# Three pooled PSUM banks for the transposes and side products of an attention kernel, assigned by a table, and back transposes in odd steps

## The reference, cut to what matters

```python
x = LN(x + L0(x))        # gated neighbour sum, all batches at once
x = LN(x + L1(x, adj))   # 4 heads + 1 output layer: softmax(mask(h h^T)) h
x = LN(x + L2(x, adj))   # softmax(mask(leaky(left_i + right_j, 0.01))) h
x = LN(x + L3(x, adj))   # the same with slope 0.2
```

## Time and profile before

| | us |
|---|---|
| median of 3 runs | 5713.18 (5706.15 to 5714.59) |
| the profiled execution | 5713.95 |
| its span, first to last instruction | 5712.2 |
| PE busy | 5265.8 (92%) |
| DVE busy | 4372.0 (77%) |
| ACT busy | 3731.8 (65%) |
| POOL busy | 1942.3 (34%) |
| mean granted clock of TensorE | 0.978 of full |

### The profile page before, as it was taken

One profiled execution on the slowest core, in us unless ns is written; L12 is line 12 of the kernel. 1 busy time (PEld: TensorE's weight loads), 2 busy tenths in 40 slices (PEclk: granted clock), 3 DMA queues, 4 the chain that ended last, 5 costly groups with the idle time before them and its releaser, 6 DMA issues.

```text
span 5712.2 us, 132229 instructions
## 1 busy us (share of the span) xinstructions
PE 5265.8 (92%) x52922; PEld 4508.6 (79%) x52922; DVE 4372.0 (77%) x7325; ACT 3731.8 (65%) x5501; POOL 1942.3 (34%) x1724
## 2 busy tenths in 40 slices
PE   8499999999999899999999999999999999999966
PEld 6388787888878788887878878787888878788755
DVE  5677678778787877778787787878788787877866
ACT  3266557676676757667576666767576675767665
POOL 3400025133341523325241343415233252413466
PEclk9799999999999999999999999999999999999988
DMA  5200000000000000000000000000000000000000
GB/s 177 61 16 11 18 9 9 9 14 14 9 9 11 17 12 7 9 18 12 15 5 10 17 14 9 9 11 16 11 9 9 18 12 15 5 9 18 13 1 5
DMA packets 138241, 95.95 MB, mean 17 GB/s; under 512 B 96032, under 2 KB 115104, under 8 KB 137632
## 3 DMA queue, kind: packets, MB, share of 16 engines
q1 hardware_dynamic: 137632, 87.49, 6.1%
HBM read 35.55 MB, written 8.91 MB: 8 GB/s over the span
## 4 chain that ended last, share of the span: by engine, by line
PE 67%; issue 12%; DVE 6%; POOLq 6%; DVEq 2%; ACT 2%; POOL 1%; DMA 0%; SPq 0%; ACTq 0%
PE po L1067 22%; PE tp L1042 22%; PE pss L1030 9%; PE pss L1031 9%; POOLq L257 6%; DVE pt L1333 3%; DVE rows L1321 2%; PE px L988 2%; DVEq L257 1%; PE px L1055 1%; PE px L1005 1%; ACT rows L1234 1%; PE px L969 1%; PE px L1015 0%; POOL shut L866 0%
## 5 line engine op out<-in xcount | busy, mean ns | idle before, releaser
L1042 PE MATMUL tp<-ident,rows 128*128 128x128 f32 x14336 | 1948.1, 278 | 234.5 <-DVE pt L1333 193.3
L1333 DVE COPY pt<-tp 128x512 f32<-128x512 f32 x2048 | 1332.8, 686 | 921.1 <-PE tp L1042 912.1
L1234 ACT ACTIVATE rows<-rows,nm 128x2048 f32<-128x2048 f32 x896 | 1795.0, 2003 | 323.3 <-DVE nm L1321 321.2
L1042 PEld LDWEIGHTS tp<-ident,rows 128*128 128x128 f32 x14336 | 1600.9, 141 | 476.8 <-issue 308.2
L1067 PE MATMUL po<-pt,hn 128*64 128x128 f32 x28672 | 1782.8, 278 | 37.5 <-ACT ot L1195 36.3
L1067 PEld LDWEIGHTS po<-pt,hn 128*64 128x64 f32 x28672 | 1568.5, 138 | 192.4 <-issue 191.7
L1186 ACT COPY pt<-tp 128x512 f32<-128x512 f32 x1536 | 837.9, 589 | 769.7 <-PE tp L1042 760.9
L869 POOL TENSOR_TENSOR rows<-sr,mask 128x2048 f32<-128x2048 f32 x256 | 1048.7, 4098 | 514.7 <-PE tp L1042 508.4
L1030 PE MATMUL pss<-ha 128*128 128x512 f32 x2560 | 1062.9, 415 | 13.1 <-DMA ha<-hb 12.0
L1031 PE MATMUL pss<-ha,hb 128*128 128x512 f32 x2560 | 1009.5, 394 | 0.0
L1321 DVE CUSTOM_DVE_ANT_0 rows<-pss,mask,nm 128x1024 f32<-128x1024 f32 x640 | 821.7, 1284 | 88.2 <-issue 3.5
(11 more groups left out here) (108 smaller groups left out, 3220.6 us busy)
## 6 DMA issues: line engine op xcount, KB each, us to landing
hb<-ha SPq DMA_DIRECT2D x164, 128.0 KB, 2.3
ha<-hb SPq DMA_DIRECT2D x164, 128.0 KB, 2.3
adjb<-in_adj SPq DMA_DIRECT2D x32, 512.0 KB, 5.6
xin<-x SPq DMA_DIRECT2D x36, 128.0 KB, 2.5
xb<-in_x SPq DMA_DIRECT2D x16, 256.0 KB, 3.0
x<-t SPq DMA_DIRECT2D x16, 256.0 KB, 2.4
xb<-x SPq DMA_DIRECT2D x8, 512.0 KB, 4.0
out<-xb SPq DMA_DIRECT2D x32, 128.0 KB, 1.9
```

What stands on the lines that cost most here:

```text
L1042: last = nc.tensor.transpose(tp[q % 2][:, r * P:(r + 1) * P], rows[:, row.slot, jb * P:(jb + 1) * P], ident[:])
L1234: nc.scalar.activation(rows[:, row.slot, :], rows[:, row.slot, :], ACT.Exp, scale=-1.0, bias=nm[:, row.place, 1:2], accum_out=rs[:, row.pl ...
L1333: nc.vector.tensor_copy(pt[:, CH * q:CH * (q + 1), row.k % SLOTS, :], tp[q % 2][:].rearrange("p (j n) -> p j n", n=P)).then_inc(pt_dve, 1)
```

## The change

`tp0`, `tp1` and `px` become a pool `ring` of three banks; PSUM is as full as before. `place_in_banks` walks once over the whole program, with a guessed time for each use (how long PE takes for it, how long until it is copied), and gives each the bank that by this guess came free first. PE waits only for the copy of that bank's last user. Back transposes go one step later, into odd steps, and all that follows from them too: `finish`, `bend_block`, `la` to `ld`, `ra`, `rb`, and in the first layers `xt`, `h`, `r`. `low`, `proj` and `hn` keep their steps. For heads, `take_sums` writes straight into `zt`, where POOL multiplies in place, so it no longer waits for POOL. The tasks ahead of the first step become a segment of their own.

```diff
-TAIL = 8
+TAIL = 9
-END_GAP = 9
+END_GAP = 10
+BANKS = 3
+SIDE = ("xn", "xt", "proj", "hn", "h", "r")
...
+    def uses(self):
+        for s in self.steps:
+            row, turned = self.row(s), self.row(s - 2)
+            yield None, (1900 if row and row.gat else 0), 0
+            for key in self.side_uses(s):
+                yield key, 600, 1300
+            for q in (0, 1):
+                if turned:
+                    yield ("turn", turned.k, q), 440, 900
+            yield None, 1950 * bool(self.odd(s - 3) or self.odd(s - 4)), 0
+            if self.back(s):
+                yield ("back", self.back(s).pair), 150, 2600
+            for key in self.side_uses(s + 0.5):
+                yield key, 600, 2600
+            for q in (2, 3):
+                if turned:
+                    yield ("turn", turned.k, q), 440, 1100
...
     def back(self, step):
-        return self.odd(step - 5)
+        return self.odd(step - 6)
     def finished(self, step):
-        return self.odd(step - 6)
+        return self.odd(step - 7)
...
         for unit in (ADD1, ADD2):
             end = at(order, unit, n + CH - 1)
-            tasks += [(end + 7, "ra", unit, c), (end + 8, "rb", unit, c)]
+            tasks += [(end + 8, "ra", unit, c), (min(end + 9, 2 * len(order) + AHEAD - 1), "rb", unit, c)]
...
+def place_in_banks(segments):
+    now, free = 0, [0] * BANKS
+    for segment in segments:
+        for key, taken, held in segment.uses():
+            if key is None:
+                now += taken
+                continue
+            bank = free.index(min(free))
+            now = max(now, free[bank]) + taken
+            free[bank] = now + held
+            assert key not in segment.bank
+            segment.bank[key] = bank
...
-        tp = [ctx.enter_context(nc.psum_tensor(f"tp{i}", [P, BANK], F32)) for i in range(2)]
+        ring = [ctx.enter_context(nc.psum_tensor(f"ring{i}", [P, BANK], F32)) for i in range(BANKS)]
         po = ctx.enter_context(nc.psum_tensor("po", [P, BANK], F32))
-        px = ctx.enter_context(nc.psum_tensor("px", [P, BANK], F32))
...
-                    nc.gpsimd.tensor_tensor(dst, ot[:], ob[:].rearrange("p r n -> p (r n)"), ALU.mult)
+                    nc.gpsimd.tensor_tensor(dst, dst, ob[:].rearrange("p r n -> p (r n)"), ALU.mult)
...
             def take_sums(row):
-                if row.pair or back_c.n:
-                    used = out_c if where[0].behind_head(row) else back_c
-                    wait(used, used.n + row.pair)
                 wait(pv_c, pv_c.n + row.pair + 1)
+                if row.unit < H:
+                    nc.scalar.copy(zt[:, row.unit, row.t // 2, :], po[:, 0:P]).then_inc(ot_ready, 1)
+                    return
+                if row.pair or back_c.n:
+                    wait(back_c, back_c.n + row.pair)
                 nc.scalar.copy(ot[:], po[:, 0:P]).then_inc(ot_ready, 1)
...
-                    finished = segment.row(s - 7)
+                    finished = segment.row(s - 8)
```

More of the change, by code:

```diff
@@ L115, in __init__, with side_uses @@
             self.tasks.setdefault(step, []).append((name, unit, c))
-        assert all(k == "before" or int(k) in self.steps for k in self.tasks), self.tasks.keys()
+        assert all(int(k) in self.steps for k in self.tasks), self.tasks.keys()
+        self.bank = {}
+    def uses(self):
[15 more added lines that the diff above has]
+                    yield ("turn", turned.k, q), 440, 1100
+    def side_uses(self, key):
+        return [task for task in self.tasks.get(key, []) if task[0] in SIDE]
     def tasks_at(self, step):
@@ L162, in prologue @@
     order = [pair for u, hn in ((0, 1), (1, 2), (2, 1), (3, 2)) for pair in pairs_of(u, hn)] + [None] * GAP
-    tasks = [("before", "xn", 0, c) for c in range(NC)]
-    tasks += [("before", name, 0, g) for g in range(2) for name in ("proj", "low", "hn")]
+    tasks = []
     for u in range(H - 1):
@@ L173, in prologue, with start @@
     return Segment(order, False, True, tasks)
+def start():
+    tasks = [(0, "xn", 0, c) for c in range(NC)]
+    return Segment([], False, False, tasks + [(0, name, 0, g) for g in range(2) for name in ("proj", "low", "hn")])
 def next_head(first):
@@ L1034, in turn @@
             def turn(row, q):
-                if q >= 2:
-                    wait_copy(row, q - 2)
-                elif row.before:
-                    wait_copy(row.before, q + 2)
+                tile = take("turn", row.k, q)
                 for r in range(CH):
                     jb = CH * q + r
-                    last = nc.tensor.transpose(tp[q % 2][:, r * P:(r + 1) * P],
+                    last = nc.tensor.transpose(tile[:, r * P:(r + 1) * P],
                                                rows[:, row.slot, jb * P:(jb + 1) * P], ident[:])
                 last.then_inc(tr_ready, 1)
+                count = copied[row.copier[q]]
+                give(count, count.n + row.count[q] + 1)
             def turn_back(row):
@@ L1073, in run_segment @@
             def run_segment(segment):
-                for task in segment.tasks.get("before", ()):
-                    run_task(*task)
+                where[0] = segment
                 for s in segment.steps:
@@ L1134, in next_of, with tile_of @@
                 wait(count)
+            where = [None]
+            def tile_of(*key):
+                return ring[where[0].bank[key]]
             def run_task(name, unit, c):
```

97 lines of the change are left out of this document (50 added, 47 removed).

## The result

| | before | after |
|---|---|---|
| median, us | 5713.06 (5706.15 to 5714.59, 5 runs) | 5739.09 (5731.19 to 5742.19, 5 runs) |
| span of the profiled execution, us | 5712.2 | 5740.3 |
| PE busy, us | 5265.8 | 5303.1 |
| DVE busy, us | 4372.0 | 4439.0 |
| mean granted clock | 0.978 | 0.968 |

The change made the kernel slower: 1.0048 times the time before, with a 95% interval of 1.0037 to 1.006. The prediction, 5655 us and faster with a chance of 0.83, had the wrong sign, and its range ended 41 us short of the result. (All times here are of undisturbed executions; one of 8962 us, at a granted clock of 0.64, is left out of a median in experiment 7.)

The account below looks back on a forecast made before the run. Outside stretches paced by POOL or ACT, PE was taken to lose time in transposes waiting for DVE's copies. Terms sum to 8.3 us a turn, 58 in seven; + 2 - 1 = 59 off 5713.95 gives 5655 us (5635 to 5670, 50%).

Parts of the forecast that it names:

- (2) of what the change costs: Steps 48 and 56: `hn` now needs group 2's bank and waits for its copy, behind `low` and bend: -2.0 us a turn.
- Odd additive steps: Nine odd additive steps outside the POOL-bound stretch: third bank lets sums stand 0.5 us earlier each, +4.5 us a turn.
- `ra` at 45, 53 and 61: `ra` goes one step later, under dot products, so DVE's copies come sooner at three steps: +3.9 us a turn.
- `la` and `ld`: Pairs move from even to odd steps, where the third bank doesn't help: -1.0 us a turn, from 0 to -3.
- Repeats at 65 and 85: Groups 2 and 3 share one bank at these steps, so the second comes later: -2.2 us a turn.
- Step 91: `proj` gets a bank ACT emptied earlier, saving its 2.43 us wait and slow sums: +3.3 us a turn, 1.3 to 3.9.
- Steps 100 to 111: POOL's wait for transposes behind late `proj` and PE's wait for `ra` shrink: +1.8 us a turn, 0 to 3.5.
- (c): Rival: norm tasks and `low` outlast dot products in odd steps, some ten places of 1.5 us: 5739 us, chance 7%.
- (e): Rival: PE's clock swings in the additive steps, eight stretches with 1.5 us more each: 5739 us, chance 2%.
- (a): Rival: the stretch of `ADD2` steps paced by POOL loosens too, its term 6.5 us a turn: 5622 us, chance 15%.
- (b): Rival: DVE takes the place of the freed bank waits, halving the +4.5 and +3.9 terms: 5685 us, chance 17%.
- (d): Rival: gains of 5 and losses of 5 cancel, or the table is in effect the old one: 5713 us, chance 9%.

Follow-up runs that it names:

- experiment 7: Kernel before with the pooled banks, heads' sums straight into `zt`, norm tasks one step later and `xt`, `h`, `r` of `ADD1` 1 to 1.5 later: 5636.0 us.
- Experiment 3: Changed kernel with `proj`, `low` and `hn` of head 2 three steps later, at 49 to 51 and 57 to 59, table made anew: 5679.9 us.
- Experiment 4: Changed kernel with `hn` of head 2 given the back transpose's bank instead of the bank of transposes' group 2: 5730.0 us.
- experiment 6: Changed kernel with each POOL mask of L911 issued as two instructions of 1024 columns: 5704.0 us.
- experiment 2: Changed kernel with its moved steps but without the bank table: groups of transposes keep two banks in turn, all else the third: 5826.9 us.
- experiment 1: Kernel before with the pool of banks and its table, all steps as before, heads' sums straight into `zt`: 5678.7 us, ratio 0.994.

## Why the prediction was wrong

**The failed step is (2) of what the change costs, steps 48 and 56: with the gains at 49 and 57, a loss of 1.0 us a turn was predicted, and 13.1 measured.** The chain in it was right: `hn` waits for the bank of group 2, DVE has `low` and the bend ahead of that copy. The duration was wrong: I priced `low` as in the earlier trace rows, where it finds POOL idle, and didn't ask where POOL's mask would be. The change moves `finish` out of the gap between two masks; that move is listed with the change, and the prediction doesn't follow it on POOL. Experiment 3 prices it: with head 2's `proj`, `low` and `hn` elsewhere, 59 us come back. Experiment 4 gives `hn` alone 9 of them, and experiment 6, where only the masks are cut, takes back 35. This term is 12.1 of the 12.5 us a turn between forecast and result; the errors of all others cancel, by luck.

The rule for it was in the prediction. The Trainium skill, "GPSIMD Engine Reference", section 1, says that GpSimd contends with VectorE instructions that read two SBUF inputs. The traces agree, with 4.46 and 3.83 us for `low` of 0.69. I applied it to the one instruction that already was slow in the trace before, the bend of the earlier trace rows, and not to the others of its kind that the change shifts against POOL.

**Odd additive steps**: +3.5 predicted for the seven, +2.9 measured. The mechanism holds: an odd step starts 0.72 us earlier, 0.17 of it because the back transpose has left the step before. At 38, 42, 54 and 62, however, 0.51 us are given back: 0.17 is the back transpose, and most of the rest a wait of groups 2 and 3 for ACT's copy, which I had put at nothing. It is the first row here, of step 41 (0.25 us). The rows behind it are steps 44 and 45, where the wait of 0.51 us of the earlier trace rows stands only at 1590.69, and the 16 transposes across the border of the steps, in one row, wait for nothing:

```profile
1577.65 0.68 PEld L1088 LDWEIGHTS ring<-ident,rows 128*128 128x128 f32 x6 [0.25 <-ACT pt L1239]
...
1590.69 1.16 PE L1088 MATMUL ring<-ident,rows 128*128 128x128 f32 x8 [0.51 <-DVE pt L1390]
...
1593.83 2.17 PE L1088 MATMUL ring<-ident,rows 128*128 128x128 f32 x16
...
1598.54 0.42 DVE L1361 TENSOR_TENSOR xb<-xb,y 128x256 f32<-128x256 f32 x1
```

**`ra` at 45, 53 and 61**: right. The 1.80 us of the earlier trace rows are gone, and these steps start 1.3 us earlier than the other odd ones. `ra` (1598.54) stands in the next step, under dot products.

**`la` and `ld`**: a loss of 1.0 predicted, a gain of 3.8 measured by step 32. I looked only at where these tasks go and not at what they leave. In the kernel before, PE waits 3.8 us a turn in steps 8 to 31, at four places: at step 16 0.59 us for ACT's copy of what `h` has just made, since a new unit begins there; at 21 and 29 `proj` and `hn` 0.69 each, until ACT has emptied `px`; and at 23 1.84 for DVE's copies. After the change 0.4 are left. The longest of the four is the tasks' own: in step 22 DVE has `ld`, `la` (its first instruction is L1291) and `low` ahead of the copies; after the change it has `lc` and `low`. Before, then after:

```profile
1468.42 0.46 DVE L1291 SCALAR_TENSOR_TENSOR y<-y 128x256 f32<-128x256 f32 x1
...
1470.94 0.85 DVE L1284 TENSOR_TENSOR ha<-hc,hb 64x512 fp32r<-64x512 f32 x1
...
1471.82 1.29 DVE L1333 COPY pt<-tp 128x512 f32<-128x512 f32 x2
...
1472.66 1.16 PE L1042 MATMUL tp<-ident,rows 128*128 128x128 f32 x8 [1.86 <-DVE pt L1333]
```

```profile
1470.68 1.29 DVE L1390 COPY pt<-ring 128x512 f32<-128x512 f32 x2
...
1472.23 1.04 PE L1088 MATMUL ring<-ident,rows 128*128 128x128 f32 x8
```

The wait at 16 goes because `h` moves to the step behind it:

```profile
1425.77 1.09 PE L1042 MATMUL tp<-ident,rows 128*128 128x128 f32 x8 [0.59 <-ACT hn L1168]
```

By step 31 the moved steps alone (experiment 2) gain 2.6 us, the banks alone 0.5: most of this gain is the moved tasks', and experiment 7 keeps it. The range of the term, 0 to -3, had no reason to end at nothing on the upper side.

**Repeats at 65 and 85**: right, 1.2 us each. The eight transposes break into two groups of four with the wait between:

```profile
1721.73 0.60 PE L1088 MATMUL ring<-ident,rows 128*128 128x128 f32 x4
1723.18 0.66 PE L1088 MATMUL ring<-ident,rows 128*128 128x128 f32 x4 [0.85 <-DVE pt L1390]
```

**Step 91**: +3.3 predicted, +1.7 measured. `proj` lost its wait of 2.43 us and the sums behind it run at 1.97 us, as foreseen. But the 1.48 us for slow sums were read from one turn and counted in all seven. Before the change the wait of 2.43 stands in every turn, and the sums behind it are slow (3.2 to 3.5 us) in the second, third and fourth only; in the others they took 1.97. And the sums of step 90 now wait for ACT, and so does the transpose behind the next back transpose:

```profile
1876.14 1.97 PE L1115 MATMUL po<-pt,hn 128*64 128x128 f32 x32 [0.56 <-ACT zt L1246]
...
1879.06 1.09 PE L1037 MATMUL ring<-xz,wts 64*64 64x128 f32 x16
...
1883.83 0.44 PE L1088 MATMUL ring<-ident,rows 128*128 128x128 f32 x2 [0.49 <-ACT pt L1239]
```

**Steps 100 to 111**: +1.8 predicted, with 0 as the lower end; -1.3 measured. POOL's masks wait less for transposes, 336.0 us in the whole program in place of 508.4, and the bend is again 2.85 us long under a mask. What the lower end left out is where it now stands: ahead of the copies of groups 2 and 3, and `proj` of step 108 has group 2's bank. Before, the transposes of step 107 waited 2.10 us behind the bend; now `proj` waits 2.71.

```profile
1976.60 4.08 POOL L911 TENSOR_TENSOR rows<-sr,mask 128x2048 f32<-128x2048 f32 x1
...
1978.11 2.85 DVE L1397 SCALAR_TENSOR_TENSOR zt<-zt 128x256 f32<-128x256 f32 x1
...
1980.88 1.28 DVE L1390 COPY pt<-ring 128x512 f32<-128x512 f32 x2
...
1981.62 6.41 PE L1037 MATMUL ring<-zt,wo 64*64 64x128 f32 x64 [2.71 <-DVE pt L1390]
```

And in this turn `proj` took 6.41 us after the wait, 3.71 in the kernel before (from 1973.51), where the clock was 1.00; its window after shows 0.56. In two more of the seven turns it took 5.38, in the other four 3.71. The sums of step 102 are slow too, 3.3 to 3.7 us in all seven turns; before, they were in four.

```profile
1973.50:1977.20 3.70, 3.70 (x66) 3.52 (x65) 3.53 (x7) 0.72 (x3) 3.70 (x2) 1.00 0.00 0
```

```profile
1981.60:1988.00 6.40, 6.38 (x65) 6.21 (x65) 3.05 (x6) 0.00 (x0) 5.46 (x5) 0.56 0.00 0
```

**The rivals.** (c), late copies in odd steps, has the measured time, 5739, and names 47 and 55 among its places. Its mechanism is not what happened: it wanted ten places at 1.5 us from `la`, `ld` and `low` outlasting the dot products. There were two at 6.6, from POOL, and the moves of `la` and `ld` gained; that the time is the same is chance. (e), the clock, was half right in kind: it didn't swing from cycling through banks (experiment 1 has the ring and a mean clock of 0.979), it fell after the two long waits. The first turn has a clock of 0.98, above the 0.97 that was named as a sign. (a), (b) and (d) are out. (In (a) the term of 6.5 doesn't follow from its words: 2.49 and twice as much are 7.5. Nothing rests on it.)

**Prologue and epilogue.** From the first `xn` to the first turn 0.5 us are gained, where 1 was predicted. The epilogue took 5.3 us longer; the banks alone made it 4.9 shorter (experiment 1), and the moved steps alone 8.2 longer (experiment 2). Where, wasn't traced further.

## What to carry to other kernels

When work moves on one engine, draw the others' long instructions over the place where it lands: in these traces a DVE instruction with two SBUF operands took its own 0.7 us only where no mask of POOL was running, and the rest of the mask besides where one was. Look at more than one turn: a slow clock seen in one of them need not be in the others. Ask of each side product that joins a shared pool of banks which copy it will wait for and what stands ahead of that copy. A change of several parts is worth taking apart: the banks gave 34 us (with the sums straight into `zt`) and the later norm tasks 43 more, and the rest of the moved steps, back transposes and finishes above all, cost 103.

## What the runs showed of the hardware

- A DVE instruction with two SBUF operands that started under one of POOL's masks (also two SBUF operands) ended behind it, in the traces of all twelve kernels and without exception (722 times): 0.54 to 0.56 us behind for `low` (512 columns), 0.28 to 0.38 for the bend and the norm pieces (256 columns). In the changed kernel these are 77 instructions. `low` of 0.69 us took 4.46, 3.83 and 2.52 us according to what was left of POOL's instruction, the bend of 0.42 us 1.45, 1.91 and 2.85.
- It is let in when the one instruction that was running ends, even if POOL has the next one ready: halving the mask nearly halved `low`.
- Which of the two starts first decides who pays. Masks under which such an instruction started took 4.07 to 4.12 us, as undisturbed ones. In the changed kernel 16 masks started while one was running, and took 4.21 to 4.55 (4.38 in the row of 1611.99).
- DVE's copies from PSUM, its scores, which read PSUM and SBUF, and its reciprocals, with one SBUF operand, weren't slowed by the masks.
- After a wait of 5.79 us, PE ran the next 2.8 us at half its clock, and eight transposes took 1.91 us in place of 1.16. The sums behind this wait at step 48 were slow in all seven turns, 2.69 to 3.56 us in place of 1.97; behind the 2.43 us of step 91, in the kernel before, they were in three of seven.
